# A fused adaLN transformer block: direct fp32/fp32r modulation matmuls, and V projection moved ahead of the softmax step

## What is computed

```python
mod = (silu(c) @ wmod).reshape(B, 6, 1, 1024)        # wmod: 1024 x 6144 fp32, 25 MB
sa, ca, ga, sb, cb, gb = mod[:, 0..5]
ga, gb = sign(ga) * max(|ga|, 0.25), sign(gb) * max(|gb|, 0.25)
h = layernorm(x) * (1 + ca) + sa
q, k, v = h @ Wq.T, h @ Wk.T, h @ Wv.T               # 16 heads of 64
sim = q @ k.T + rel_bias                             # causal
x = x + ga * (softmax(sim) @ v) @ Wo.T
h = layernorm(x) * (1 + cb) + sb
x = x + gb * ((round(h * s) / s) @ ternary_W.T)      # one scale s a row
```

## Time and profile before

| | us |
|---|---|
| runs before | 1312.9 and 1318.92, median 1315.91 |
| profiled execution, its own time | 1314.82 |
| its span on core 5, the slowest | 1312.9 |
| spans of the 8 cores | 1292.0 to 1312.9 |
| TensorE busy | 763.6 (58%) |
| VectorE busy | 572.5 (44%) |
| ScalarE busy | 427.4 (33%) |

### The profile page before, as it was taken

One profiled execution on the slowest core, in us unless ns is written; L12 is line 12 of the kernel. 1 busy time (PEld: TensorE's weight loads), 2 busy tenths in 40 slices (PEclk: granted clock), 3 DMA queues, 4 the chain that ended last, 5 costly groups with the idle time before them and its releaser, 6 DMA issues.

```text
span 1312.9 us, 16544 instructions; the slowest of 8 cores (1292.0 to 1312.9 us)
## 1 busy us (share of the span) xinstructions
PE 763.6 (58%) x3853; PEld 314.2 (24%) x3853; DVE 572.5 (44%) x1333; ACT 427.4 (33%) x849; POOL 126.0 (10%) x214
## 2 busy tenths in 40 slices
PE   0211542318887887988878887888488200111198
PEld 0000210004343333433333333332133000000043
DVE  0236641233234243333434334243388257555567
ACT  0001300010655635466363654637200201333300
POOL 1111210001111111111121100000000022000000
PEclk9999999999798898978889897887799655555599
DMA  8853156802101111011110200000000000000023
GB/s 262 205 111 78 15 114 176 277 2 40 12 8 29 13 24 15 9 30 10 28 13 8 30 7 17 1 17 1 17 1 1 16 16 0 1 0 0 1 107 149
DMA packets 47924, 61.12 MB, mean 47 GB/s; under 512 B 33389, under 2 KB 38573, under 8 KB 44760
## 3 DMA queue, kind: packets, MB, share of 16 engines
q1 hardware_dynamic: 14254, 33.24, 8.3%
q0 software_dynamic: 28896, 8.42, 6.3%
q10 hardware_dynamic: 4682, 18.41, 4.7%
HBM read 58.31 MB, written 10.14 MB: 52 GB/s over the span
## 4 chain that ended last, share of the span: by engine, by line
PE 47%; DVE 23%; DMA 14%; issue 9%; ACT 5%; DVEq 1%; ACTq 1%; SPq 0%
PE p_o L729 15%; PE p_s L621 9%; PE p_s L690 7%; PE p_v L649 5%; DMA swmF<-wm 5%; PE p_f L947 4%; DMA srep<-dtaus 4%; DVE soT L599 2%; ACT sPt L705 2%; PE p_s L792 2%; DMA sx<-x 2%; PE p_v L655 2%; DVE stats6b L267 2%; DVE stats6b L264 2%; PE p_tr L923 2%
## 5 line engine op out<-in xcount | busy, mean ns | idle before, releaser
L705 ACT ACTIVATE sPt<-p_s 128x512 bf16<-128x512 f32 (+3 forms) x640 | 297.9, 535 | 248.1 <-PE p_s L690 243.9
L729 PE MATMUL p_o<-sPt,sv 128*65 128x512 bf16 (+3 forms) x640 | 230.1, 411 | 95.6 <-DVE soT L763 36.6
L660 DVE CAST sv<-p_v 128x128 bf16<-128x128 f32 x128 | 37.7, 295 | 239.9 <-PE p_v L655 235.9
L690 PE MATMUL p_s<-sqt,skt 64*128 64x512 bf16 (+3 forms) x640 | 126.3, 406 | 7.0 <-DVE skt L628 7.0
L923 PE MATMUL p_tr<-sid,sy 128*128 128x128 bf16 x128 | 25.0, 271 | 180.3 <-DVE sy L918 161.1
L729 PEld LDWEIGHTS p_o<-sPt,sv 128*65 128x65 bf16 x640 | 66.0, 117 | 220.7 <-issue 210.7
L402 PE MATMUL p_mod<-swmB,scsilb 128*1 128x512 bf16 x96 | 44.6, 621 | 90.1 <-DVE swmB L398 90.1
L649 PE MATMUL p_v<-swv,shT 128*128 128x128 bf16 x1024 | 86.4, 232 | 0.2 <-DVE sv L660 0.2
L649 PEld LDWEIGHTS p_v<-swv,shT 128*128 128x128 bf16 x1024 | 73.0, 105 | 16.3 <-issue 9.0
L713 DVE TENSOR_TENSOR sPt<-sPt,sE 128x240 bf16<-128x240 bf16 (+1 forms) x256 | 60.8, 266 | 35.9 <-ACT sPt L705 31.4
L792 PE MATMUL p_s<-swo,soT 128*128 128x512 bf16 x256 | 62.3, 387 | 24.3 <-DVE soT L599 15.7
(11 more groups left out here) (102 smaller groups left out, 801.8 us busy)
## 6 DMA issues: line engine op xcount, KB each, us to landing
swmF<-wm ACTq DMA_DIRECT2D x16, 1024.0 KB
sx<-x SPq DMA_DIRECT2D x16, 512.0 KB
swmF<-wm SPq DMA_DIRECT2D x8, 1024.0 KB
out<-sx SPq DMA_DIRECT2D x16, 512.0 KB
srbt<-dsumB SPq DMA_DIRECT2D x16, 256.0 KB
swq<-wq POOLq DMA_DIRECT2D x64, 32.0 KB, 2.1
swk<-wk POOLq DMA_DIRECT2D x64, 32.0 KB, 2.1
swv<-wv POOLq DMA_DIRECT2D x64, 32.0 KB, 2.1
```

Source lines behind the costliest of these rows:

```text
L660: sq.add("vector", lambda e, t=t, vb=vb, pv=pv: e.tensor_copy(sv4[:, vb, t, :, 0:64], pv[:].rearrange("p (g c) -> p g c", c=64)), reads=[p ...
L690: o=o, qc=qc: e.matmul(pb[:, qoff:512], skt[o:o + 64, 128 * kt:128 * (kt + 1)], sqt[o:o + 64, 512 * qc + qoff:512 * (qc + 1)], start=True, ...
L705: hb=hb: e.activation(sPt[:, sl, hb, qoff:512], pb[:, qoff:512], AF.Exp, bias=EXPB, scale=F1),
L729: sl=sl, nkt=nkt, vb=vb: e.matmul(p_o2[hb][:, qoff:512], sv[:, vb, kt, 65 * hb:65 * hb + 65], sPt[:, sl, hb, qoff:512], start=(kt == 0), s ...
```

## The change

Two edits.

The first is in `mod_group`. The bf16 copies and the VectorE cast are gone. Group 0 loads fp32 into `swm0` (issued by ScalarE as before) and multiplies in fp32 by `scsil0`. Groups 1 and 2 load into `swm`, declared fp32r, from GpSimd, and multiply in fp32r by `scsil`. `swm0` and `swm` are separate, two buffers each. A chunk's buffer is now read by the matmuls, so the DMA two chunks later waits for them and not for a cast. In GpSimd's order the 16 DMAs of groups 1 and 2 stand behind `wload(1)` and ahead of those of `wo`.

The second is in the attention loop. A V group, its VectorE copy included, is put between `emit_qk` of the next key tile and `emit_sm`/`emit_pv` of this one; before it stood behind them.

```diff
-            swmB = sb1("swmB", [128, 2, 2048], BF16)
-            swmF = sb1("swmF", [128, 2, 2048], F32)
-            scsilb = sb1("scsilb", [128, 8], BF16)
+            swm = sb1("swm", [128, 2, 2048], F32R)
+            swm0 = sb1("swm0", [128, 2, 2048], F32)
+            scsil0 = sb1("scsil0", [128, 8], F32)
...
             def mod_group(jg):
-                qe = ("scalar", "sync", "scalar")[jg]
+                qe = ("scalar", "gpsimd", "gpsimd")[jg]
+                tile = swm0 if jg == 0 else swm
+                col = scsil0 if jg == 0 else scsil
+                ctag = "csil0" if jg == 0 else "csil"
+                wtag = "swm0" if jg == 0 else "swmr"
                 for c in range(NCH):
                     p = (NCH * jg + c) % 2
-                    sq.add(qe, lambda e, jg=jg, c=c, p=p: e.dma_start(
-                        out=swmF[:, p, :],
+                    sq.add(qe, lambda e, jg=jg, c=c, p=p, tile=tile: e.dma_start(
+                        out=tile[:, p, :],
                         in_=wm[128 * c:128 * (c + 1), 2048 * jg:2048 * (jg + 1)]),
-                        writes=[f"swmF:{p}"], dma=True)
-                    sq.add("vector", lambda e, p=p: e.tensor_copy(
-                        swmB[:, p, :], swmF[:, p, :]),
-                        reads=[f"swmF:{p}"], writes=[f"swmB:{p}"])
+                        writes=[f"{wtag}:{p}"], dma=True)
...
-                            scsilb[:, c:c + 1],
-                            swmB[:, p, 512 * sl:512 * (sl + 1)],
+                            col[:, c:c + 1],
+                            tile[:, p, 512 * sl:512 * (sl + 1)],
...
-                        for hb in (0, 1):
-                            emit_sm(hb, kt)
-                            emit_pv(hb, kt)
                         step_idx[0] += 1
                         if vsteps:
                             want = (step_idx[0] * len(vsteps)) // TOT
                             while vinj[0] < want:
                                 vsteps[vinj[0]]()
                                 vinj[0] += 1
+                        for hb in (0, 1):
+                            emit_sm(hb, kt)
+                            emit_pv(hb, kt)
```

More of the change, by code:

```diff
@@ L365, in build_nc @@
                    reads=["sil"], writes=["csil"])
-            sq.add("vector", lambda e: e.tensor_copy(scsilb[:], ssil[:]),
-                   reads=["sil"], writes=["csilb"])
+            sq.add("vector", lambda e: e.tensor_copy(scsil0[:], ssil[:]),
+                   reads=["sil"], writes=["csil0"])
             sq.add("tensor", lambda e: e.matmul(p_gen[0:16, 0:128], srel[:], soh[:],
@@ L390, in mod_group @@
             def mod_group(jg):
-                qe = ("scalar", "sync", "scalar")[jg]
+                qe = ("scalar", "gpsimd", "gpsimd")[jg]
[3 more added lines that the diff above has]
+                wtag = "swm0" if jg == 0 else "swmr"
                 for c in range(NCH):
                     p = (NCH * jg + c) % 2
-                    sq.add(qe, lambda e, jg=jg, c=c, p=p: e.dma_start(
-                        out=swmF[:, p, :],
+                    sq.add(qe, lambda e, jg=jg, c=c, p=p, tile=tile: e.dma_start(
+                        out=tile[:, p, :],
                         in_=wm[128 * c:128 * (c + 1), 2048 * jg:2048 * (jg + 1)]),
-                        writes=[f"swmF:{p}"], dma=True)
-                    sq.add("vector", lambda e, p=p: e.tensor_copy(
-                        swmB[:, p, :], swmF[:, p, :]),
-                        reads=[f"swmF:{p}"], writes=[f"swmB:{p}"])
+                        writes=[f"{wtag}:{p}"], dma=True)
                     for sl in range(4):
-                        sq.add("tensor", lambda e, c=c, sl=sl, p=p: e.matmul(
+                        sq.add("tensor", lambda e, c=c, sl=sl, p=p, tile=tile,
+                               col=col: e.matmul(
                             p_mod[:, 512 * sl:512 * (sl + 1)],
-                            scsilb[:, c:c + 1],
-                            swmB[:, p, 512 * sl:512 * (sl + 1)],
+                            col[:, c:c + 1],
+                            tile[:, p, 512 * sl:512 * (sl + 1)],
                             start=(c == 0), stop=(c == NCH - 1)),
-                            reads=["csilb", f"swmB:{p}"],
+                            reads=[ctag, f"{wtag}:{p}"],
                             writes=[f"p_mod:{sl}"])
```

## The result

| | before | after |
|---|---|---|
| median of the timed executions | 1313.68 (42) | 1316.33 (43) |
| ratio of the medians | | 1.0028, interval 1.0014 to 1.0041 |
| slowest core's span, profiled execution | 1312.9 | 1315.6 |
| TensorE busy | 763.6 | 788.5 |
| VectorE busy | 572.5 | 540.5 |

The change costs 3.7 us (1.8 to 5.4). That lies inside the predicted range and inside "no change" as the text defined it, but on the other side of zero from the 3.5 us gain that the sum gave. So the question of this study is a sum of terms that nearly cancel: which were right, and which turned its sign.

The account below looks back on a forecast made before the run. No single engine was taken to bound the kernel; each stretch was read by itself. Stage 1 (+5 - 7 + 2.5 = +0.5 us) and attention (-4) summed to -3.5 on 1314.8, giving 1311; range 1288 to 1334, the forecast's own 1300 to 1322.

Parts of the forecast that it names:

- Half clock, -3: Attention loop: TensorE's three 1.2 GHz stretches a pair shrink by 0.4 us a pair, -3 us.
- the attention part as forecast (-4): Attention loop: filled waits less masked-step losses give -1 us, shorter half-clock stretches -3, together -4 us.
- Unmasked steps, -16: Attention steps without mask: the V group fills TensorE's wait before P@V, -2.3 us a pair, some 16 in all.
- Masked steps, +15: Masked attention steps: V copy ahead of the mask makes TensorE stand 0.8 us; +2.15 us a pair, some 15.
- Rival C: Masked attention steps: the next masked P@V also goes on waiting 0.57 us; +28 us, 1339; chance 0.10.
- Block start: Starts of attention blocks 2 and 3: the long TensorE wait shrinks from 2.98 to about 2.1 us.
- rival D: Attention blocks 2 and 3: half-clock stretches at their starts go; -31 us, 1280; chance 0.13.
- Group 0, +5: Stage 1, group 0: fp32 matmuls without cast take 5.8 us a chunk against 4.97; +5 us.
- Rival A: Stage 1, group 0: fp32 is dear, 7.4 us a chunk at 1.2 GHz; +12 over forecast, 1323; chance 0.15.
- Tables, group 2 and `wo`: Stage 1, later groups: bias tables still set the pace; group 2 gains 7 us, `wo` beside gate rows costs 2.5.
- rival B: Stage 1, groups 1 and 2: GpSimd's slow queue sets the end, break-even 5.3 us a chunk; 1328 to 1391; chance 0.10.

Follow-up runs that it names:

- e1: First edit alone (fp32 and fp32r modulation matmuls) on the kernel before: 1310.16 us, ratio 0.9987 to before.
- e13: Unchanged repeat of e1, the first edit alone: 1314.34 us, ratio 1.0001 to before.
- e5: First edit alone, but group 0 left in bf16 with the VectorE cast: 1304.87 us, ratio 0.9939 to before.
- e6: First edit alone, with all 16 bias tables issued by SyncE, none by ScalarE: 1299.65 us, ratio 0.9908 to before.
- e16: Kernel before, with five extra ScalarE operations of 1.06 us ahead of stage 2: 1315.24 us, ratio 1.0006 to before.
- e2: Second edit alone (V groups, copy included, ahead of P@V) on the kernel before: 1310.70 us, ratio 0.9989 to before.
- e14: Unchanged repeat of e2, the second edit alone: 1316.16 us, ratio 1.0003 to before.
- e12: The whole changed kernel run again, unchanged: 1316.12 us, ratio 1.0023 to before.
- e15: The whole changed kernel run once more, unchanged: 1316.05 us, ratio 1.0025 to before.
- e8: Changed kernel, with five extra ScalarE operations of 1.06 us ahead of stage 2: 1320.25 us, ratio 1.0062 to before.
- e4: Second edit only in the unmasked V steps, masked ones in the old order, on the kernel before: 1297.09 us, ratio 0.9873 to before.
- e3: Second edit alone, but the VectorE copy of each V group behind its step's masks and P@V: 1277.06 us, ratio 0.9715 to before.
- e11: Whole changed kernel, but the VectorE copy of each V group behind its step's masks and P@V: 1280.02 us, ratio 0.9736 to before.
- e7: Kernel before, with the scaling of the previous pair's `soT` behind the copies that free `p_o`: 1260.59 us, ratio 0.9594 to before.

## Why the prediction was right and wrong

**Half clock, -3: the step that failed.** The sentence was "Half clock: three stretches a pair ... I count 0.4 us a pair, -3". It looked only at stretches that were there, only for what would shrink, and took all seven pairs as alike. What the runs show instead are stretches that were not there. Pair 0 has no `soT` to scale, so in before its blocks start without the 3 us wait. By core, the medians of pair 0 are:

| V groups | pair 0, us | of it at half clock, us |
|---|---|---|
| as before: before, e1, e13, e5, e6, e16 | 72.9, 72.1, 72.7, 72.0, 72.4, 72.1 | 10.2, 6.8, 10.2, 6.8, 8.5, 6.8 |
| V edit whole: e2, e14, after, e12, e15, e8 | 78.8, 78.8, 78.7, 77.9, 77.9, 77.2 | 23.9, 23.9, 23.9, 20.5, 18.8, 17.1 |
| V edit in unmasked steps: e4 | 70.4 | 6.8 |
| V edit, copy behind: e3, e11 | 70.5, 69.5 | 13.7, 10.2 |

Six executions against six, without overlap: 6 us. The text had named a move of over 2 us in a pair as what would prove it wrong. The windows over the end of block 2 and the start of block 3 of pair 0 (the share after POOL's is the granted clock), of after:

```profile
357.00:361.00 4.00, 3.39 (x22) 1.35 (x21) 1.20 (x5) 3.11 (x8) 0.53 (x1) 1.00 0.11 14
361.00:365.00 4.00, 2.68 (x16) 1.65 (x16) 1.62 (x8) 0.45 (x2) 1.06 (x2) 0.59 0.09 8
365.00:369.00 4.00, 3.20 (x13) 1.12 (x14) 1.37 (x2) 3.25 (x7) 0.53 (x1) 0.50 0.17 16
369.00:373.00 4.00, 4.00 (x19) 1.39 (x16) 0.29 (x1) 2.35 (x5) 1.05 (x2) 0.63 0.09 8
```

and of before, the same place in the work:

```profile
358.00:362.00 4.00, 3.22 (x23) 1.48 (x22) 2.07 (x9) 2.49 (x8) 1.05 (x2) 1.00 0.10 12
362.00:366.00 4.00, 2.89 (x22) 1.37 (x22) 1.58 (x4) 3.35 (x7) 0.53 (x1) 1.00 0.17 16
366.00:370.00 4.00, 3.89 (x29) 1.70 (x27) 0.29 (x1) 3.61 (x8) 1.05 (x2) 1.00 0.10 9
```

In after TensorE stands in front of masked P@Vs of this place for 0.40, 0.74 and 0.68 us (timeline of after):

```profile
359.12 0.86 PE L731 MATMUL p_o<-sPt,sv 128*65 128x512 bf16 x2 [0.40 <-DVE sPt L715]
...
361.64 0.77 PE L731 MATMUL p_o<-sPt,sv 128*65 128x384 bf16 x2 [0.74 <-DVE sPt L715]
...
364.94 0.45 PE L731 MATMUL p_o<-sPt,sv 128*65 128x128 bf16 x2 [0.68 <-DVE sPt L715]
```

and the granted clock falls to 0.50 at about the second of them, for some 10 us, where this core of before kept 1.00. On six of the eight cores of after two shorter stretches of 3.4 us come in as well, at the start of block 2 and in the projection behind the pair. e4 and e3, which leave the V groups of masked steps or just their copies where they were, don't have the longer pair 0, and e4 differs from e2 in nothing else. So the edit in the masked steps is what brings the stretches in.

They don't bring them in every time. On core 6 of e2 TensorE stands for the same 0.40, 0.74 and 0.68 us in the same place, and the clock stays at 1.00. One row of its timeline, then its windows:

```profile
356.00 0.51 PE L729 MATMUL p_o<-sPt,sv 128*65 128x384 bf16 x2 [0.74 <-DVE sPt L713]
```

```profile
355.00:359.00 4.00, 2.59 (x23) 1.65 (x22) 2.00 (x9) 1.15 (x5) 0.53 (x1) 1.00 0.11 12
359.00:363.00 4.00, 2.83 (x21) 1.16 (x18) 1.28 (x3) 3.79 (x8) 0.53 (x1) 1.00 0.18 16
```

That gives a test within one kernel. The 48 cores of the six executions with the V edit whole, ordered by how long pair 0 was at half clock: 3.4 us, pair 0 takes 72.5; 10.2, 74.5; 13.7, 75.8; 17.1, 77.2; 20.5, 78.6; 23.9, 78.9 (medians of 3, 2, 6, 9, 2 and 26 cores). With the V groups as before: 6.8 us, 72.0; 10.2, 72.7; 13.7, 74.0; 17.1, 74.7 (27, 11, 5 and 5 cores). At equal half clock the V edit costs some 2 us, so of the 6 some 4 are the clock and some 2 the standing itself.

The sum of the attention part, by the means of the six and six medians: the text had -0.55 a pair for pairs 0 to 6. Pair 0 made +5.9 of it (72.4 to 78.2), pairs 1 to 6 together -1.1 (472.1 to 470.9) where the text had -3.3, and pair 7 +1.1 (52.3 to 53.4) where it had nothing. The 6.4 us of pair 0 are most of the distance between the attention part as forecast (-4) and as measured (+6 in before and after, +5 in these means).

In the other pairs a half-clock piece can move to another place. In after the Q/K projection behind a pair took 13.9 us where the clock was full, as it always was in the steady pairs of before, and about 1.7 more where the clock fell within it. Rows of the chain in order of time (start, length, what), of after:

```profile
467.61 15.61 PE p_s L623 x64
...
784.62 13.90 PE p_s L623 x64
```

A pair with such a projection had 3.4 us of half clock in the projection and 13.7 in its steps, where before had 20.5 in the steps, and took 78.3 to 78.6 us. Pairs of after with 20.5 us in the steps and none in the projection took no longer (core 5, 78.4 to 78.8). So "three stretches a pair at 0.50" held roughly in pairs 1 to 6 (109 us in six pairs), but not in pair 0, where before had one and after has four.

**Unmasked steps, -16.** Right: -16.7 timed, -17.2 in the loop (e4). In kind it is less clean than the sum of waits said. The step's own gain is seen, 0.87 and 1.59 us a step, but in e4 the time at half clock fell too, from 155 to 133 us, worth up to 11. Waits filled and clock regained can't be told apart by these runs.

**Masked steps, +15.** Right in size, +15.2 timed and +17.9 in the loop (e4 to e2), but this is partly luck: 8.4 of the 17.9 are pair 0, where the new stretches are, and a price for those was not in the 15. In the steps of other pairs the mechanism is as described: 0.73 of standing against 0.8 predicted, none in the next P@V. Rival C had said that the next one goes on waiting; it doesn't.

**Block start.** 1.93 us where the text expected about 2.1, and the clock fell all the same. "2.1 us of standing still is still much" held, and so rival D did not come. e7 shows the other side: at 0.8 to 0.9 us of wait it did.

**Group 0, +5.** Measured +8.2 (e1 and e13 +8.4 and +9.4). The pace of after was forecast at 5.8 us a chunk and is 6.0 (median over the seven cores whose records are complete, first matmul to first matmul). That two errors against each other made it come out so is luck. The middle value for the matmuls, 5.3 us, was too high: 3.59 to 5.02 on the slowest core, and a median of 3.7 over the cores from a chunk's first matmul to the issue that its end releases. The landing was too low: 6.4 us as in an empty kernel, where the median from issue to matmul is 7.5. What was mis-sized is the pace of before: core 5 has 4.97 us a chunk, the median core 4.8. Over 7 distances that makes +8.3 instead of +6; the first matmul came 1.1 earlier, as forecast. By the four passes that the Trainium skill gives for true fp32 (FP8 and Floating Point Precision, TensorE Precision Notes) the estimate was 3.4 us a chunk at 2.4 GHz; the trace agrees, with 3.59. Rival A was wrong because it held the clock at 1.2 GHz: the granted clock rose within the first two chunks, in which TensorE was busy without a gap (9.71 us).

**Tables, group 2 and `wo`.** Group 1 is late by 2.9 (222.5 to 225.4), where the text handed on the whole delay of group 0: the chain of the bias tables took up the rest. Group 2 comes 32.2 us behind group 1, 40.3 before (medians): -8.1 for -7 predicted. The fp32r chunks of group 2 came 4.08 us apart (242.28 to 262.69 over 5), 4.3 predicted and under the 5.3 of break-even, so rival B is out. The gate rows beside `wo` cost +5.2 instead of +2.5 (31.4 to 36.6 from the first copy of group 2 to the first projection). 2.9 - 8.1 + 5.2 is 0 where the text had +0.5: its errors (-2.1, -1.1, +2.7) cancelled too.

**What stays open.** Six loops with the V groups as before took 594.2 to 599.2 with nothing edited in them, and four of after (e8 with them) 601.3 to 605.2. The V edit alone gave 599.9 and 599.7, and by the times it cost nothing (0.9989, 1.0003), since its pairs 1 to 6 took 469 instead of 470 to 474. After did not keep that (472.4): its second and sixth pair and its last, whose code is the same in both, were 1.7, 1.6 and 2 us longer. Whether this is an effect of the two edits together or of how the loop's start falls, the runs can't tell. Nor do they show what decides on which cores the same waits lower the clock. So pair 0 is shown as the place where the forecast of the attention part failed, but that the change as a whole lost 3.7 us while each half alone shows no loss is not explained; the intervals leave room for chance.

## What to carry to other kernels

When a sum consists of terms that cancel, price also what isn't there yet: look at the stretches at full clock and ask which added waits, each below a microsecond, would stand close together in them. Look at the first repetition of a loop by itself; it can lack a wait that all the others have. And compare the cores of one execution: where the same code takes different times on them, the clock's part can be read off. If matmuls are put earlier, keep their evacuating copy where it was: an engine that works in order should have the operation that someone waits for (here the mask) ahead of the one that nobody needs soon. And at a block's end do first what frees the accumulator, then the scaling that is needed only much later; that was worth 4%, some fourteen times what the change had moved.

## What the hardware showed

- An fp32 product of a single column with 128 x 512 is recorded as two matmuls. Four such products took 3.59 us at a granted clock of 1.00. The same four in fp32r took 1.86 us at a granted clock of 0.50, as in bf16. At an equal clock fp32 is then about four times as dear (an estimate from the two figures: 3.59 against half of 1.86).
- Loads of 1 MB in fp32 into an fp32r tile from GpSimd's queue, two in flight, came 4.08 us apart in group 2 and 4.50 in group 1 (198.25 to 220.74 over 5, core 1), where bias tables were loaded beside them. The Trainium skill (DMA: Bandwidth & Descriptors, Bandwidth) lists 6.15 us for one issued from GpSimd; with two in flight the trace is below that.
- Waits of 0.40, 0.74 and 0.68 us within 6 us, of a TensorE that otherwise worked, were followed by a granted clock of 0.50 for some 10 us on six of the eight cores of after. On core 6 of e2 the same three waits left it at 1.00.
- One kernel gave loops of 594.2 and 599.2 us in two executions on different chips (e1, e13), and another 605.2, 603.1 and 602.2 (after, e12, e15). A few microseconds between two profiled executions are no verdict on an edit within the loop.
